# One row sum instead of two in an attention stage: GpSimd adds the DMA engines' partial sum to its own, and waits at the stage borders are split

## The chip, the core and the metric

The kernel runs on one core of a Trainium2 chip. The engines of the core are TensorE (PE, matmuls), VectorE (DVE), ScalarE (ACT), GpSimd (POOL) and SyncE (SP, which here only issues transfers); each works through its own queue in order, and they meet at semaphores. The metric is the device time of one execution in microseconds. Before the change it is 3310.89 us, the median of 3 runs (3309.64 to 3310.94).

## What is computed

```python
x = L0_attn_x                       # (2, 2048, 1024)
xn = _layernorm(x)
q, k, v = xn @ wq, xn @ wk, xn @ wv # 32 heads of 32, 8 key heads, each for 4 query heads
scores = q k^T * 32 ** -0.5, causal
s = (softmax(scores) @ v) @ wo
w = top 2 of 8 experts, softmax(xn @ W_router.T), renormalised
base = xn @ W_base.T + b_base
g = silu(base + 2.0 * sum_e w_e * (xn @ lora_A[e].T) @ lora_B[e].T)
return x + s * g
```

## The kernel before, in words

The 4096 tokens are eight chunks of 512 (CH). Four stages follow each other on one core, and TensorE works in all of them.

1. Constants: a block of its own (L1556) in which POOL makes an identity and two masks and DVE rounds two of them. The next block starts when all engines have left it.
2. Projection (project_programs, L251): for each chunk the weights, split in a high and a low half for accuracy, are multiplied with the turned tokens (three products, L596 to L598), v and router first, then eight q products, two k products and one for the adapters. The results go through DRAM. During the last chunk the first score products of the attention stage are mixed in (scores_to, maxima_to and move_rows; SCORES_OF is how many for each product, LEAD = 84 in all). load_ahead (L1156) fetches the first k, v and q for it.
3. Attention: 16 groups (a batch and a key head with its four query heads), each with chunks c = 0 to 3 of 512 queries. In chunk c there are 4(c+1) tiles of 128 keys, j. A table (EVENTS, L166, filled by rule for each tile) sets the order of the work on all engines alike: PE multiplies scores twice, once with queries in rows for the maxima ("S", L1284, row_max on DVE, a group ahead), once with keys in rows for the exponentials ("T", L1380; ACT writes probs, L1441). "W" multiplies probs with v (L1335).
   The sum of the exponentials over the keys is formed in three ways. ADDS (L145) lists the tiles that POOL adds into added (L1249, op "A"); DMA_ADDS (L146) lists those that a DMA with an add sums into dma_added (L1259, op "D", issued by POOL, each waiting for the landing of the one before); REST names four tiles of chunk 3 that nobody adds. "Y" (row_sums, L1340) lets PE multiply added, dma_added and the rest with ones (L1353) for a chunk's sum. It stands 18 tiles into the next chunk, for chunk 3 behind tile 9 of the next group.
   After Y, ACT copies the sum, SyncE moves it into few columns (L1), DVE inverts it ("I"), SyncE stores (L2, L1213) and spreads it (L3, L1220), POOL multiplies o_sb with it ("N", L1272), and SyncE stores the result (L4, L1225) when the multiply is done. In SyncE's queue L4 of chunk 3 (tile 41 of the next group) stands ahead of L2 and L3 of chunk 0 (tiles 45 and 49).
   The probs live in a ring of 11 buffers; ACT waits for a buffer until its last reader is done.
4. Gate (gate_programs, L654) and output projection (L829). The gate's weights are split by ACT (high, L717) and DVE (low, L756) into gw; first_products (L807) works on the first tokens before the last row sum.

## Time and profile before

| | |
|---|---|
| median of 3 runs | 3310.89 us |
| profiled execution | 3312.78 us, span 3311.0 us |
| PE busy | 3238.1 us (98%) |
| DVE, ACT, POOL busy | 1889.5, 1437.3, 1357.0 us |
| attention stage | about 682 to 2574 us |

Busy time counts instructions of the engine alone, not the ones that issue transfers or wait. A busy PE is not PE at its peak, since matmuls are pipelined and their ends are modelled: the distance between two starts says more than a duration. Idle time of another engine costs nothing by itself; what matters is who waits for whom.

### The profile page before, as it was taken

How to read it: one execution, taken by the hardware profiler on the slowest of the kernel's cores; microseconds unless marked ns; L12 is line 12 of the kernel's file. 1: busy time of each engine (PE TensorE's matmuls, PEld its weight loads, DVE VectorE, ACT ScalarE, POOL GpSimd, SP SyncE). 2: the span in 40 equal slices, each digit the busy share in tenths (PEclk: the TensorE clock that was granted, in tenths of full speed). 3: DMA queues.
4: the chain of work that ended last, by engine and by line, in shares of the span. 5: the costliest groups of instructions: out<-in, count | busy, mean ns of one | idle time of the engine just before them, and what ended most of it. 6: DMA issues, size and time to landing. Idle time of an engine off the chain costs nothing.

```text
span 3311.0 us, 51264 instructions
## 1 busy us (share of the span) xinstructions
PE 3238.1 (98%) x18048; PEld 2193.0 (66%) x18048; DVE 1889.5 (57%) x4622; ACT 1437.3 (43%) x2658; POOL 1357.0 (41%) x549
## 2 busy tenths in 40 slices
PE   6999999999999999999999999999999999999999
PEld 5888888755555555555555555555553788888887
DVE  6333333577777777777777777777773322223333
ACT  3222111056666666666666666666666111010110
POOL 0000000046776776776686677678667000000000
PEclk9999999999999999999999999999999999999999
DMA  6455554556666666566566666666666544445554
GB/s 232 158 163 158 166 159 147 143 119 132 143 137 135 143 130 138 125 142 138 128 145 138 137 136 129 138 132 145 135 162 142 174 140 138 144 156 191 192 199 165
DMA packets 283503, 494.53 MB, mean 149 GB/s; under 512 B 40864, under 2 KB 156576, under 8 KB 263328
## 3 DMA queue, kind: packets, MB, share of 16 engines
q1 hardware_dynamic: 260256, 333.04, 33.7%
q0 software_dynamic: 20736, 151.00, 23.2%
q10 hardware_dynamic: 2304, 7.87, 0.7%
q8 instruction: 113, 1.85, 0.2%
q14 instruction: 94, 0.77, 0.1%
HBM read 205.03 MB, written 134.74 MB: 103 GB/s over the span
## 4 chain that ended last, share of the span: by engine, by line
PE 91%; DVE 4%; ACT 1%; DMA 1%; issue 1%; SPq 1%; POOL 0%; ACTq 0%; DVEq 0%; POOLq 0%
PE cols_ps L1380 16%; PE o_ps L1335 15%; PE rows_ps L1284 14%; PE cols_ps L596 4%; PE cols_ps L598 4%; PE cols_ps L597 4%; PE cols_ps L1353 4%; PE rows_ps L795 4%; PE rows_ps L796 4%; PE rows_ps L797 4%; PE rows_ps L947 4%; PE rows_ps L946 4%; PE rows_ps L945 4%; DVE row_max L1469 2%; PE cols_ps L1383 2%; PE o_ps L596 1%
## 5 line engine op out<-in xcount | busy, mean ns | idle before, releaser
L1249 POOL TENSOR_TENSOR added<-added,probs 128x2048 f32<-128x2048 f32 (+3 forms) x320 | 1171.7, 3661 | 859.2 <-PE o_ps L1335 793.0
L1469 DVE TENSOR_REDUCE row_max<-rows_ps 128x1 f32<-128x512 f32 x1536 | 994.8, 683 | 297.8 <-PE rows_ps L1284 294.7
L1441 ACT ACTIVATE probs<-cols_ps 128x512 f32<-128x512 f32 x1728 | 919.1, 610 | 305.6 <-PE cols_ps L1380 278.6
L1473 DVE CUSTOM_DVE_ANT_0 masked_rows<-rows_ps,tri 128x128 bf16<-128x128 f32 (+3 forms) x1024 | 484.5, 483 | 176.7 <-PE rows_ps L1284 174.1
L1284 PE MATMUL rows_ps<-k_st,q_st 96*128 96x512 f32 (+3 forms) x1536 | 520.7, 362 | 12.8 <-DVE row_max L1469 7.9
L1380 PE MATMUL cols_ps<-q_st,k_st 97*128 97x512 f32 x1248 | 519.8, 423 | 6.7 <-issue 6.1
L1335 PE MATMUL o_ps<-probs,v_st 128*32 128x512 f32 (+3 forms) x4224 | 428.6, 522 | 0.0
L1380 PE MATMUL cols_ps<-q_st_last,k_st 97*128 97x512 f32 x928 | 381.3, 425 | 4.4 <-ACT dma_added L1441 3.2
L1284 PE MATMUL rows_ps<-k_st,q_st_last 96*128 96x512 f32 (+3 forms) x1024 | 364.5, 381 | 2.0
L1380 PEld LDWEIGHTS cols_ps<-q_st,k_st 97*128 97x128 f32 x1248 | 236.7, 190 | 179.7 <-issue 113.0
L1284 PEld LDWEIGHTS rows_ps<-k_st,q_st 96*128 96x128 f32 x1536 | 292.7, 191 | 91.0 <-DVE row_max L1469 36.9
L1380 PEld LDWEIGHTS cols_ps<-q_st_last,k_st 97*128 97x128 f32 x928 | 174.4, 189 | 151.2 <-issue 88.7
L1259 POOL DMA_DIRECT2D dma_added<-probs x144 | 125.8, 874 | 315.6 <-ACT probs L1441 308.3
L1335 PEld LDWEIGHTS o_ps<-probs,v_st 128*32 128x32 f32 x4224 | 111.3, 109 | 209.8 <-issue 145.0
L596 PE MATMUL cols_ps<-xt_hi,w_hi 128*128 128x512 f32 x576 | 231.8, 402 | 0.6 <-DVE logits L531 0.6
L795 PE MATMUL rows_ps<-gw,g_t 128*128 128x512 f32 x576 | 225.1, 391 | 6.6 <-DVE gw L756 5.0
L1284 PEld LDWEIGHTS rows_ps<-k_st,q_st_last 96*128 96x128 f32 x1024 | 194.2, 190 | 53.5 <-DVE row_max L1469 20.5
L598 PE MATMUL cols_ps<-xt_hi,w_lo 128*128 128x512 f32 x576 | 227.7, 395 | 0.0
L597 PE MATMUL cols_ps<-xt_lo,w_hi 128*128 128x512 f32 x576 | 227.3, 395 | 0.0
L797 PE MATMUL rows_ps<-gw,g_t 128*128 128x512 f32 x576 | 224.6, 390 | 0.0
L796 PE MATMUL rows_ps<-gw,g_t 128*128 128x512 f32 x576 | 224.6, 390 | 0.0
L1441 ACT ACTIVATE added<-cols_ps 128x512 f32<-128x512 f32 x256 | 139.3, 599 | 146.4 <-PE cols_ps L1380 109.2
(130 smaller groups left out, 3862.7 us busy)
## 6 DMA issues: line engine op xcount, KB each, us to landing
dma_added<-probs POOLq DMA_DIRECT2D x144, 1024.0 KB, 7.8
q_st<-scratch_q_hi SPq DMA_DIRECT2D x96, 256.0 KB, 6.0
x_sb<-in_x SPq DMA_DIRECT2D x32, 512.0 KB, 4.1
scratch_xt_hi<-xt_hi SPq DMA_DIRECT2D x32, 512.0 KB, 6.0
scratch_xt_lo<-xt_lo SPq DMA_DIRECT2D x32, 512.0 KB, 6.7
scratch_q_hi<-out_hi SPq DMA_DIRECT2D x64, 256.0 KB, 2.5
scratch_q_lo<-out_lo SPq DMA_DIRECT2D x64, 256.0 KB, 2.9
l_sb<-scratch_l_inv SPq DMA_DIRECT2D x256, 64.0 KB, 4.8
```

The costliest lines, as they stand in the source:

```text
L596: nc.tensor.matmul(out, lh, rh, start=(k == 0), stop=False)
L597: nc.tensor.matmul(out, lh, rl, start=False, stop=False)
L598: ins = nc.tensor.matmul(out, ll, rh, start=False, stop=(k == KT - 1))
L795: nc.tensor.matmul(acc[half][:, :], t_hi, w[:, k, 0, cols], start=(k == 0), stop=False)
L796: nc.tensor.matmul(acc[half][:, :], t_hi, w[:, k, 1, cols], start=False, stop=False)
L1249: nc.gpsimd.tensor_tensor(total[:, :, q0:CH], total[:, :, q0:CH], probs_of(c, j)[:, :, q0:CH], ALU.add).then_inc(pool_added, 1)
L1284: nc.tensor.matmul(rows_ps[rows_slot(k)][:, 0:keys], q_st[c][0:K1, h, i * P:(i + 1) * P], k_st[kbuf][0:K1, CH * p:CH * p + keys], start=Tr ...
L1335: ins = nc.tensor.matmul(o_ps[h * HD:(h + 1) * HD, q0:CH], v_st[vbuf][:, j, :], probs_of(cc, j)[:, h, q0:CH], start=(j == 0), stop=(j == s ...
L1380: ins = nc.tensor.matmul(into, k_st[n.u][:, j * P:(j + 1) * P], q_st[c][:, :, i * P:(i + 1) * P], start=True, stop=not diagonal)
L1441: nc.scalar.activation(probs_of(c, j)[:, :, i * P:(i + 1) * P], cols_ps[cols_slot(AT_T[t])][:, :].rearrange("p (h q) -> p h q", h=NREP), A ...
L1469: nc.vector.tensor_reduce(into, bank[:, :], AX.X, ALU.max).then_inc(rows_free, 1)
L1473: nc.vector.tensor_tensor_reduce(masked_rows[rows_slot(k)][:, 0:keys], bank[:, 0:keys], tri[:, CH - keys:CH], 1.0, MASKED, ALU.add, ALU.ma ...
```

## The change

GpSimd gets one more kind of operation, "J": after its last add of a chunk that has DMA adds (chunks 1 to 3), it waits for the last of these to land and adds dma_added to added. PE's row sum no longer reads dma_added. At the borders of the stages waits become finer: the constants are made at the start of the one large block; the first v products are ordered by weight row, each waiting for its own; the last chunk's scores start one product later, nine to a product; v is loaded behind q and the last q before the last stores; PE waits only for the accumulators that the next tiles need; the gate's first products take all high halves before the low ones.

```diff
-SCORES_OF = KT
+SCORES_OF = KT + 1
...
+    if DMA_ADDS[_c]:
+        event(max(tiles_through(_c, ADDS[_c][-1]) - 1, weighed_at(_c, ADDS[_c][0])), "J", _c)
...
-NADD = sum(len(a) - 1 for a in ADDS if a)
+JOINED = [1 if a else 0 for a in DMA_ADDS]
+NADD = sum(len(a) - 1 for a in ADDS) + sum(JOINED)
...
+            def join(n, c, back):
+                total = added[c % 2]
+                added_of, par = dma_adds_through(c, NJG), c % 2
+                pool.wait_ge(dma_done[par], n.lin(16 * NDMA[par], 16 * (added_of - back * NDMA[par])))
+                pool.wait_ge(pool_added, n.lin(NADD, sums_through(c) - 1 - back * NADD))
+                nc.gpsimd.tensor_tensor(total[:, :, :], total[:, :, :], dma_added[par][:, :, :], ALU.add).then_inc(pool_added, 1)
...
-                pe.wait_ge(pool_added, n.lin(NADD, adds_through(cc, NJG) - back * NADD))
+                pe.wait_ge(pool_added, n.lin(NADD, sums_through(cc) - back * NADD))
                 parts = [(added[cc % 2], 0)]
-                if DMA_ADDS[cc]:
-                    added_of, par = dma_adds_through(cc, NJG), cc % 2
-                    pe.wait_ge(dma_done[par], n.lin(16 * NDMA[par], 16 * (added_of - back * NDMA[par])))
-                    parts.append((dma_added[cc % 2], 0))
...
-        pe.wait_ge(w_lo_ready, KT)
...
-                for t in range(TPC):
+                if first_pair and u == 0:
+
+                    pe.wait_ge(acc_free, TPC)
+                    for k in range(KT):
+                        pe.wait_ge(w_lo_ready, k + 1)
...
-                    scored = SCORES_OF * (j - 1)
-                    between = None if ahead or j == 0 else lambda k: scores_to(scored + k + 1)
+                    scored = SCORES_OF * (j - 2)
+                    between = None if ahead or j < 2 else lambda k: scores_to(scored + k + 1)
...
-                load_kv(0, 0)
+                load_k(0, 0)
                 load_q(0, 0)
                 load_q(0, 1)
                 load_q(0, 2)
+                load_v(0, 0)
...
-            pe.wait_ge(project.acc_free, project.acc_free_last)
-            pe.wait_ge(ones_ready, 2)
+            pe.wait_ge(project.acc_free, project.acc_free_last - 2)
+            pe.wait_ge(ones_ready, 1)
...
+                        if n.lin(1) == 0 and t == 2:
+
+                            pe.wait_ge(project.acc_free, project.acc_free_last)
+                        if n.lin(1) == 1 and t == 0:
+                            pe.wait_ge(ones_ready, 2)
...
+        for k in range(NW):
+            pe.wait_ge(w_hi_ready, k + 1)
+            for part in range(2):
+                for half in range(2):
+                    nc.tensor.matmul(acc[half][:, :], tokens[0][:, part, k, :], w[:, k, 0, halves[half]],
+                                     start=(k == 0 and part == 0), stop=False)
         for k in range(NW):
             pe.wait_ge(w_lo_ready, k + 1)
             for half in range(2):
-                ins = step(0, half, k)
+                ins = nc.tensor.matmul(acc[half][:, :], tokens[0][:, 0, k, :], w[:, k, 1, halves[half]], start=False,
+                                       stop=(k == NW - 1))
```

The order on GpSimd's queue at the end of chunk 1 and the start of chunk 2, group 1. Before (added1 and dma_added1 are the partial sums of chunk 1, added0 and dma_added0 those of chunk 2, o_sb3 belongs to chunk 3 of the group before, o_sb0 to chunk 0):

```order
L1249 TENSOR_TENSOR added1<-added1,probs7 128x4x256
L1249 TENSOR_TENSOR added1<-added1,probs8 128x4x128
L1272 TENSOR_TENSOR o_sb3<-o_sb3,l_sb1 128x512
L1259 DMA dma_added0<-probs9 128x2048
L1249 TENSOR_TENSOR added0<-added0,probs10 128x2048
L1272 TENSOR_TENSOR o_sb0<-o_sb0,l_sb0 128x512
L1259 DMA dma_added0<-probs0 128x2048
```

And in the changed kernel, at the same place:

```order
L1332 TENSOR_TENSOR added1<-added1,probs7 128x4x256
L1332 TENSOR_TENSOR added1<-added1,probs8 128x4x128
L1340 TENSOR_TENSOR added1<-added1,dma_added1 128x2048
L1364 TENSOR_TENSOR o_sb3<-o_sb3,l_sb1 128x512
L1349 DMA dma_added0<-probs9 128x2048
L1332 TENSOR_TENSOR added0<-added0,probs10 128x2048
L1364 TENSOR_TENSOR o_sb0<-o_sb0,l_sb0 128x512
L1349 DMA dma_added0<-probs0 128x2048
```

One row is new, the add of dma_added1, and it stands ahead of the multiply of the chunk before and of the first DMA add of the next chunk.

The order on TensorE at the row sum of chunk 3, before (probs7 to probs10 are the four tiles that nobody adds):

```order
L1353 MATMUL cols_ps1<-added1,ones 32x512 x4
L1353 MATMUL cols_ps1<-dma_added1,ones 32x512 x4
L1353 MATMUL cols_ps1<-probs7,ones 32x512 x4
L1353 MATMUL cols_ps1<-probs8,ones 32x384 x4
L1353 MATMUL cols_ps1<-probs9,ones 32x256 x4
L1353 MATMUL cols_ps1<-probs10,ones 32x128 x4
```

And in the changed kernel:

```order
L1443 MATMUL cols_ps1<-added1,ones 32x512 x4
L1443 MATMUL cols_ps1<-probs7,ones 32x512 x4
L1443 MATMUL cols_ps1<-probs8,ones 32x384 x4
L1443 MATMUL cols_ps1<-probs9,ones 32x256 x4
L1443 MATMUL cols_ps1<-probs10,ones 32x128 x4
```

The row on dma_added is gone; the place of the sum among the tiles is the same.

## Rows read from the trace of the kernel before

**Rows 1.** The page, busy time, share and instructions of each engine
```profile
PE 3238.1 (98%) x18048; PEld 2193.0 (66%) x18048; DVE 1889.5 (57%) x4622; ACT 1437.3 (43%) x2658; POOL 1357.0 (41%) x549
```
**Rows 2.** Windows: stretch, length; busy PE, PEld, DVE, ACT, POOL; granted clock; DMA; GB/s
```profile
720.00:2500.00 1780.00, 1760.60 (x10976) 993.05 (x10974) 1341.50 (x3576) 1144.05 (x2186) 1281.97 (x501) 1.00 0.63 137
...
2515.00:2550.00 35.00, 34.05 (x158) 11.29 (x150) 0.25 (x1) 21.96 (x45) 27.18 (x12) 0.91 0.56 118
...
601.00:606.40 5.40, 5.35 (x15) 4.39 (x16) 1.71 (x8) 0.00 (x0) 0.00 (x0) 0.50 1.07 223
```
**Rows 3.** The chain of waits from 720 to 2500 us, by line
```profile
by line: PE cols_ps L1380 27.8%; PE o_ps L1335 27.2%; PE rows_ps L1284 25.2%; PE cols_ps L1353 7.0%; DVE row_max L1469 4.4%; PE cols_ps L1383 3.0%; DVE masked_rows L1473 1.9%; ACT dma_added L1441 1.2%; issue 1.1%; ACT o_sb L1457 0.5%; PE ro
```
**Rows 4.** Timeline, one row sum: start, us, engine, line, operation, operands, count
```profile
729.29 1.04 PE L1353 MATMUL cols_ps<-added,ones 128*32 128x512 f32 x8
...
730.15 1.04 PE L1353 MATMUL cols_ps<-dma_added,ones 128*32 128x512 f32 x8
```
**Rows 5.** Timeline of POOL, group 1; in brackets the idle time before
```profile
834.67 3.82 POOL L1249 TENSOR_TENSOR added<-added,probs 128x1024 f32<-128x1024 f32 x2
838.45 1.28 POOL L1272 TENSOR_TENSOR o_sb<-o_sb,l_sb 128x512 f32<-128x512 f32 x1
...
852.36 1.28 POOL L1272 TENSOR_TENSOR o_sb<-o_sb,l_sb 128x512 f32<-128x512 f32 x1 [4.34 <-ACT probs L1441]
853.58 0.86 POOL L1259 DMA_DIRECT2D dma_added<-probs  x1
...
864.32 12.49 POOL L1249 TENSOR_TENSOR added<-added,probs 128x2048 f32<-128x2048 f32 x4
...
878.01 0.87 POOL L1259 DMA_DIRECT2D dma_added<-probs  x1
...
886.58 0.87 POOL L1259 DMA_DIRECT2D dma_added<-probs  x1 [3.09 <-ACT probs L1441]
...
911.54 4.88 POOL L1249 TENSOR_TENSOR added<-added,probs 128x2048 f32<-128x2048 f32 x1
```
**Rows 6.** Timeline of SyncE's queue, the same group
```profile
839.82 0.36 SPq L1225 DMA_DIRECT2D scratch_o<-o_sb  x1
840.30 0.37 SPq L1213 DMA_DIRECT2D scratch_l_inv<-l_few  x1
843.41 4.16 SPq L1220 DMA_DIRECT2D l_sb<-scratch_l_inv  x4
```
**Rows 7.** Timeline of PE: three row sums begin
```profile
805.94 1.04 PE L1353 MATMUL cols_ps<-added,ones 128*32 128x512 f32 x8
...
881.13 1.04 PE L1353 MATMUL cols_ps<-added,ones 128*32 128x512 f32 x8
...
923.19 1.04 PE L1353 MATMUL cols_ps<-added,ones 128*32 128x512 f32 x8
```
**Rows 8.** Timeline of POOL, group 0
```profile
760.14 0.87 POOL L1259 DMA_DIRECT2D dma_added<-probs  x1 [1.44 <-ACT probs L1441]
...
795.00 4.87 POOL L1249 TENSOR_TENSOR added<-added,probs 128x2048 f32<-128x2048 f32 x1
```
**Rows 9.** The page, DMA issues: count, size, median us to landing
```profile
dma_added<-probs POOLq DMA_DIRECT2D x144, 1024.0 KB, 7.8
```
**Rows 10.** Timeline of SyncE's queue, start
```profile
5.71 1.82 SPq L312 DMA_DIRECT2D x_sb<-in_x  x4
```
**Rows 11.** Timeline of PE, waits at the borders
```profile
49.74 0.50 PE L596 MATMUL cols_ps<-xt_hi,w_hi 128*128 128x512 f32 x1 [0.62 <-DVE logits L531]
...
601.05 0.48 PE L1284 MATMUL rows_ps<-k_st,q_st 96*128 96x128 f32 x1 [4.86 <-DMA q_st<-scratch_q_hi]
...
681.62 0.77 PE L1380 MATMUL cols_ps<-q_st,k_st 97*128 97x512 f32 x1 [6.05 <-issue]
...
2559.32 0.77 PE L795 MATMUL rows_ps<-gw,g_t 128*128 128x512 f32 x1 [5.00 <-DVE gw L756]
```
**Rows 12.** The line's instructions: count, ns min/median/max, first and last start
```profile
L756 DVE TENSOR_TENSOR gw<-gw_raw,gw x9: 1210/1211/5485, 2553.7 to 2567.0; 128x1024 fp32r<-128x1024 f32 x9
```

More of the change, by code:

```diff
@@ L371, in pair_of_chunks @@
                     store_xt(Step(pair, 1) if u == 0 else Step(pair + 1, 0), 1 - u)
+                if last and u == 1:
+                    wait_apart(sp, acc_full, NA * NCH - 1, passed)
+                    wait_apart(sp, xt_stored[1], 16 * 2 * TPC * (NCH // 2 + 1), passed)
+                    load_last()
                 s = (NO * u + NO - 1) % 2
@@ L605, in tensor, with pair_of_chunks @@
             turn(zero, j)
-        pe.wait_ge(w_lo_ready, KT)
-        def pair_of_chunks(pair, b, last):
+        def pair_of_chunks(pair, first_pair, last):
             for u in range(2):
@@ L620, in pair_of_chunks @@
                 pe.wait_ge(turn_free, n.lin(NTR, NTR + 4))
-                for t in range(TPC):
+                if first_pair and u == 0:
+                    pe.wait_ge(acc_free, TPC)
+                    for k in range(KT):
+                        pe.wait_ge(w_lo_ready, k + 1)
+                        (wh, wl) = weights(k, C_V, C_Q)
+                        for t in range(TPC):
+                            (th, tl) = tokens(k, t * P, (t + 1) * P)
+                            into = acc[t][:, C_V:C_Q]
+                            nc.tensor.matmul(into, th, wh, start=(k == 0), stop=False)
+                            nc.tensor.matmul(into, th, wl, start=False, stop=False)
+                            ins = nc.tensor.matmul(into, tl, wh, start=False, stop=(k == KT - 1))
+                            if k == KT - 1:
+                                ins.then_inc(acc_full, 1)
+                for t in () if first_pair and u == 0 else range(TPC):
                     pe.wait_ge(acc_free, n.lin(NA, t + 1))
@@ L636, in pair_of_chunks @@
                         turn(m, j)
-                    if not ahead and j > 0:
+                    if not ahead and j > 1:
                         scores_to(scored + SCORES_OF)
@@ L647, in pair_of_chunks @@
                 ins.then_inc(acc_full, 1)
-        over_chunks(pe, pair_of_chunks)
-    Project = namedtuple("Project", "sync gpsimd scalar vector tensor acc_free acc_free_last acc_hi acc_hi_last")
-    return Project(sync, gpsimd, scalar, vector, tensor, acc_free, NA * NCH + 4, acc_hi, NA * NCH)
+        pair_of_chunks(0, True, False)
+        with pe.Fori(1, 3) as pair:
+            pair_of_chunks(pair, False, False)
+        pair_of_chunks(3, False, True)
+    Project = namedtuple("Project", "sync all_stored gpsimd scalar vector tensor acc_free acc_free_last acc_hi acc_hi_last")
+    return Project(sync, all_stored, gpsimd, scalar, vector, tensor, acc_free, NA * NCH + 4, acc_hi, NA * NCH)
 def gate_programs(nc, ctx, sc, wo, b_base, w_raw, w, ow_raw, ow_hi, ow_lo, tokens, bias, z, th, g, acc, passed):
@@ L809, in first_products @@
         pe.wait_ge(t_loaded[0], 64)
+        halves = [slice(half * HALF, (half + 1) * HALF) for half in range(2)]
+        for k in range(NW):
[4 more added lines that the diff above has]
+                                     start=(k == 0 and part == 0), stop=False)
         for k in range(NW):
@@ L1057, in all_stages @@
         NW = KT + 1
+        made = sem("made")
+        rounded = sem("rounded")
+        constants = constants_programs(nc, ident, ident_r, plain_ji, mask_ji, tri, made, rounded)
         project = project_programs(nc, ctx, x, wall, sc, ident, work, small, cols_ps + [o_ps], rows_ps)
@@ L1160, in load_ahead @@
                 load_q(0, 2)
+                load_v(0, 0)
             moved = [0]
             def move_rows(end):
-                for k in FIRST_ROWS[moved[0]:end]:
+                for k in FIRST_ROWS[moved[0]:max(end, 0)]:
                     if ROWS[k][0] == "M":
@@ L1168, in move_rows, with load_last @@
                 moved[0] = max(moved[0], min(end, len(FIRST_ROWS)))
-            project.sync(sp, load_ahead, move_rows)
+            def load_last():
+                load_q(0, CPB - 1)
+            project.sync(sp, load_ahead, move_rows, load_last)
             assert moved[0] >= max(i for i, k in enumerate(FIRST_ROWS) if ROWS[k][0] == "M")
@@ L1184, in run @@
                             wait_apart(sp, probs_ready, made_count(n, c - 1, 0, NJG) if c else n.lin(NUG, 0), passed)
-                        if c == 0 or not last_group:
+                        if c == 0 and n.lin(1) == 1:
+                            project.all_stored(sp)
+                        if c == 0 and n.lin(1) == 0:
+                            pass
+                        elif c == 0 or not last_group:
                             load_q(n.lin(1, 0 if c == 0 else 1), (c - 1) % CPB)
@@ L1265, in run @@
                         add(n, *op[1:])
+                    elif op[0] == "J":
+                        join(n, *op[1:])
                     elif op[0] == "D":
@@ L1273, in run @@
                             .then_inc(norm_ready, 1)
+            constants.gpsimd(pool)
             project.gpsimd(pool)
@@ L1297, in scores_to @@
             def scores_to(end):
-                for k in FIRST_ROWS[scored[0]:end]:
+                for k in FIRST_ROWS[scored[0]:max(end, 0)]:
                     free = rows_free_count(None, 0, k) if k >= NROWS else None
@@ L1493, in maxima_to @@
             def maxima_to(end):
-                for k in FIRST_ROWS[done[0]:end]:
+                for k in FIRST_ROWS[done[0]:max(end, 0)]:
                     count = rows_count(None, 0, k)
@@ L1504, in maxima_to @@
                 done[0] = max(done[0], min(end, len(FIRST_ROWS)))
+            constants.vector(dve)
             project.vector(dve, begin_maxima, maxima_to)
```

65 lines of the change are left out of this document (35 added, 30 removed).

## The prediction

> **What bounds the kernel now.** I read the page's busy shares first [rows 1], then the stages by windows, the chain of waits, and last GpSimd's, SyncE's and TensorE's own timelines. TensorE (PE) is busy 98% of the span. In the attention stage it is busy 1760.6 of 1780 us [rows 2], and the chain of waits lies on its products for over 90% of that stretch [rows 3]. So work taken off PE there is worth its full time, if nothing else becomes late. GpSimd (POOL) looks half idle (41%), and that is misleading: its idle time lies in holes between links of a chain. Below I follow one of the 16 groups through its chunks 1 to 3, because the change loads exactly that engine.
>
> **What is removed.** After a row sum's eight records on `added` come eight on `dma_added`, 729.29 then 730.15 [rows 4]: 0.86 us per part. The engine is never idle there, so nothing hides the part. Chunks 1 to 3 of 16 groups have such a part, 48 sums: 48 x 0.86 = 41.3 us off PE.
>
> **What is added.** 48 joins of 128x2048 on POOL. The same form of add takes 4.6 us: four adds of 2048, 1536, 1024 and 512 elements, two and a half of them in work, take 12.49 us, the row at 864.32 [rows 5]; I keep 4.57. 48 x 4.6 = 220 us on an engine that is busy 1357 of 3311 us [rows 1]: it fits in total. The question is what is queued behind each join, and for that I retime group 1 of [rows 5], in the clock of before:
>
> Join of chunk 1: the adds end at 838.5, the last DMA add of the chunk, issued 8.4 us before that, has just landed (7.8 us in the median) [rows 9], so the join runs 838.8 to 843.4. Behind it on POOL stands the multiply of o_sb of the chunk before (838.45), now done at 844.6 instead of 839.7. SyncE's queue waits for that multiply: its store went out at 839.82, and behind it in the same queue stand the store of the inverse sums (840.30) and the spread of them (843.41) [rows 6]. All three move by some 5 us. The spread feeds the next multiply on POOL (852.36), where POOL already sits idle 4.34 us (the row names probs, but in its queue it is the multiply that waits for the spread); this becomes 857.2. The multiply blocks the DMA add at 853.58, now 858.4, so 4.85 us late. From 853.58 to 876.8 POOL is gapless, so all of it arrives.
>
> Join of chunk 2: runs 881.8 to 886.3, while TensorE comes to that sum at 881.13, less the 0.86 saved before it [rows 7]. PE waits about 5.5 us. Then the multiply, then chunk 3's first DMA add, at 887.6 instead of 878.01.
>
> Join of chunk 3: here POOL and the DMA adds are one chain, each DMA add waiting for the landing of the one before (878.01 and 7.8 to land, and 0.8 to be noticed, give 886.58), with adds filling the rest; the adds end at 916.4, 38.4 us after that first DMA add. Started at 887.6, they end at 926.0 and the join at 930.7. TensorE comes to the sum at 923.19 - 1.7 saved + 5.5 already waited = 927.0. It waits another 3 us or more.
>
> So group 1 saves 2.6 us and waits some 8. It is a bad one. In other groups the spread has slack before it is needed. Done in the same way for all 15 groups that have a successor, the two waits together come to 1.1 us in the mildest and 8.2 in the worst, 74 us in sum. A rough control: chunk 3's adds end on average 6.7 us before their sum begins (in the first 6.1: add from 795.00, sum at 805.94 [rows 7, 8]; over the 15 groups 4.4 to 8.1). Against that stand the join 4.6, the push by chunk 2's join (4.6 less the 1.44 us of idle time at 760.14 [rows 8]) 3.1, the sums that come 1.7 earlier, and the push from chunk 1 through SyncE, between 0 and 4.9, say 2.3 on average: 11.7 - 6.7 = 5.0 a group, 75 us. Bounds: 0 if the joins find holes, 38 if the push through SyncE does not reach POOL, 105 if each DMA add lands 0.5 us later than its median of 7.8 [rows 9]. I take 74, since all terms come from rows of this very chain. Attention stage: -41.3 + 74 = +33 us.
>
> The Trainium skill (DMA: Bandwidth & Descriptors, Anatomy of one DMA) fits such a transfer as 2 us plus bytes at 436 GB/s, by my estimate 4.4 us for 1 MB. The row says 7.8, so by the page chunk 3's chain would have 6 us more slack and the sum would come out near the second rival.
>
> **The start.** SyncE's first load stands at 5.71 us [rows 10], behind the block of the constants. Without that block it can go out at about 1.4 us, 4.3 us earlier; DVE's two copies of constants still end before the tokens land. The first weights are multiplied as they arrive, but the next product waits for DVE's logits, at 49.74 [rows 11], and DVE is busy with the split of the weights and the statistics whatever PE does. So this earlier work gains nothing, and PE then idles about 9 us, after which its granted clock is at the low level, as it was for the 5.4 us behind the 4.86 us wait at 601 (0.50 of full, 1.2 GHz) [rows 2, 11]: that stretch cost about 2.4 us. Net -2.0, bounds -4.3 and 0.
>
> **Border to attention.** PE waited 4.86 us for q_st at 601.05 and then ran until 606.4 at the low clock [rows 2, 11], 2.4 us lost. With the scores one product (5.5 us) later and k and q loaded before v, both go: -7.2 (bounds -7.2 and -4). The 81 scores now share 9 products instead of 10, DVE's load per product rises to some 7.2 of 7.4 us: just hidden. Next, PE's 6.05 us before 681.62 [rows 11]: it may start two tiles at once, but then needs DVE to free the score banks, and DVE has the last low half and a memset of one row of k_st in front of that, until about 681.5; it is late next. I take -2 (bounds -6 and 0).
>
> **Border to the gate.** PE waited 5.0 us for the first low part of gw [rows 11] and then had a stretch of low clock like the one at 601, but shorter; I put it at 1.5 us lost. That first subtraction took 5485 ns where its like take 1211 [rows 12]: it stood still until POOL's add ended. With the high halves first PE has 8.3 us of work without it. But now POOL has, after its late add, another multiply, add and join, 10.6 us, and DVE 9 subtractions, 10.9 us; if they exclude each other, both are over only near 2579, where the sum of chunk 3 began at 2573.2. I take +3 (bounds -7 and +6).
>
> The Trainium skill (SBUF — State Buffer, Who interferes with whom) calls the shared port an exclusive lock between a GpSimd read and a DVE instruction with two SBUF inputs; the 5485 ns agree. By it the saving here is given back; without it the term would be -6.
>
> **Sum.** -41.3 + 74 - 2.0 - 7.2 - 2.0 + 3 = +24.5 us on the profiled execution (span 3311.0, whole 3312.78): 3337. The median of the runs is 1.9 us lower: 3335.4, say 3336.
>
> **The rivals.**
> 1. The joins are hidden. For it speaks POOL's 41%; against it the 6.7 us of slack against a join of 4.6 with 3.1 in front. -41.3 - 8.2 = 3261. Chance 8%.
> 2. On the other side, one mechanism: only chunk 3's chain is late, the push through SyncE's queue does not reach POOL's DMA adds, since the spread lands sooner once it no longer meets other transfers. The waits are then 38.6 us; from below 49.5 us in sum the kernel is faster than before. -41.3 + 38.6 - 8.2 = 3300. Against it: the 4.34 us hole in front of 852.36. Chance 22%.
> 3. As forecast, and TensorE's clock falls at the longer waits. In the last group, with less than 1 us of PE idle in 35, the granted clock averaged 0.91 [rows 2], so 9% of full speed was lost there without a long wait. Some 25 waits at 0 to 2.4 us (the loss at 601) are 0 to 60 us; a third is 20 us, 3356. Chance 13%.
> 4. Waits of 45 to 57 us in sum, neither case clean: 3310, no change. Chance 9%.
>
> **The numbers.** The forecast has 48%, its own range 3318 to 3356. A change under 0.2% (6.6 us) can't be told from none. Faster: 8 + 19 of the second rival = 27%. Same: 10%. Slower: 63%. The range 3290 to 3366 leaves out the first rival and the far end of the third.
>
> **What would show it.** A PE wait released by `added` in front of the row sums of chunk 2 and above all chunk 3, some 5 us a group, absent at chunks 0 and 1. The distance from POOL's first DMA add of chunk 3 to the end of its adds still near 38 us, and the multiply behind the join of chunk 1 about 5 us later against the adds. PE's row-sum records 384 fewer. A group's period, 117.25 us now, near 119.5. At 601 no wait; the first load 4.3 us earlier. Wrong would be a period of 114.7 (rival 1), or a wait on DVE or ACT in place of the one on POOL.

## The result, and the profile after

The changed kernel takes 3364.1 us (median of 4 runs, 3360.9 to 3368.7), the kernel before 3310.9 in the same session: ratio 1.0161, 95% interval 1.0147 to 1.0175. The forecast was 3336, slower by 25; it is slower by 53. The direction was right and the size was not; of the waits, which the forecast put above all at chunk 3, 48.8 us stand at chunk 2 and 14.2 at chunk 3. The profiled execution took 3368.7 us, its span is 3366.9 against 3311.0, so 55.9 us are to be explained.

The page first: busy time, share and instructions of each engine, and the start of the chain that ended last, by engine.

```profile
PE 3238.3 (96%) x17664; PEld 2199.7 (65%) x17664; DVE 1896.5 (56%) x4622; ACT 1439.7 (43%) x2658; POOL 1576.9 (47%) x597
...
PE 74%; POOL 11%; DMA 6%; issue 4%; DVE 3%; ACT 2%; SPq 0%; ACTq 0%; POOLq 0%; DVEq 0%
...
L1340 POOL TENSOR_TENSOR added<-added,dma_added 128x2048 f32<-128x2048 f32 x48 | 219.8, 4580 | 12.2 <-DMA dma_added<-probs 5.9
```

TensorE has 384 instructions fewer and yet the same busy time as before [rows 1]; stretches of low clock, below, gave back what the removed ones took off. Of the chain it was 91% before, now GpSimd and the DMA engines hold 17% of it. The join is as long as forecast, 4.58 us.

The attention stage, by windows (stretch, length, busy PE, PEld, DVE, ACT, POOL, granted clock, DMA share, GB/s), and the largest waits of TensorE and of GpSimd's multiply in the same stretch (sum in us, times, longest).

```profile
720.00:2500.00 1780.00, 1699.66 (x10276) 971.33 (x10279) 1303.52 (x3481) 1111.82 (x2117) 1448.15 (x530) 0.98 0.62 132
```
```profile
POOL o_sb L1364 <- DMA l_sb<-scratch_l_inv: 70.1, 12, 7.5
PE cols_ps L1443 <- POOL added L1340: 61.4, 23, 5.6
```

Against [rows 2] TensorE stands 61 us more, all of it in front of the joined sums, and its mean clock is 0.98, not 1.00. GpSimd, the engine that is late, itself stands 70 us in front of its multiply and waits there for the spread. Group 1 on GpSimd, SyncE and TensorE (start, length, engine, line; in brackets the idle time before):

```profile
835.07 4.59 POOL L1340 TENSOR_TENSOR added<-added,dma_added 128x2048 f32<-128x2048 f32 x1 [1.24 <-DMA dma_added<-probs]
839.62 1.29 POOL L1364 TENSOR_TENSOR o_sb<-o_sb,l_sb 128x512 f32<-128x512 f32 x1
840.85 0.85 POOL L1349 DMA_DIRECT2D dma_added<-probs  x1
...
853.15 1.27 POOL L1364 TENSOR_TENSOR o_sb<-o_sb,l_sb 128x512 f32<-128x512 f32 x1 [6.84 <-DMA l_sb<-scratch_l_inv]
...
877.74 4.49 POOL L1340 TENSOR_TENSOR added<-added,dma_added 128x2048 f32<-128x2048 f32 x1
...
921.04 4.60 POOL L1340 TENSOR_TENSOR added<-added,dma_added 128x2048 f32<-128x2048 f32 x1
```
```profile
841.01 0.36 SPq L1308 DMA_DIRECT2D scratch_o<-o_sb  x1
841.48 0.45 SPq L1296 DMA_DIRECT2D scratch_l_inv<-l_few  x1
848.61 2.82 SPq L1303 DMA_DIRECT2D l_sb<-scratch_l_inv  x4
```
```profile
844.16 1.04 PE L1443 MATMUL cols_ps<-added,ones 128*32 128x512 f32 x8
...
882.38 1.93 PE L1443 MATMUL cols_ps<-added,ones 128*32 128x512 f32 x8 [4.35 <-POOL added L1340]
...
925.82 1.04 PE L1443 MATMUL cols_ps<-added,ones 128*32 128x512 f32 x8
```

The forecast chain can be read off link by link: join, multiply, SyncE's store, the store of the inverse sums, the spread, the multiply of chunk 0, the adds, the join of chunk 2, TensorE's wait. One link is new. The store of the inverse sums (8 KB) needs 7 us to land (the spread behind it goes out at 848.61); before it needed 3 (840.30 to 843.41, [rows 6]).

The 55.9 us by stretches, read from the start of the same TensorE instruction in both traces:

| stretch | forecast | measured |
|---|---|---|
| start, to the second turning of tokens (55.40, now 54.30) | -2.0 | -1.1 |
| TensorE at 345 to 352 us | 0 | +5.9 |
| border to attention, to the first row sum (707.10, now 702.51) | -9.2 | -9.4 |
| first row sum to that of the last group (1759.5, now 1814.3 us) | +35.3 | +54.8 |
| last group with the border to the gate (106.6, now 112.8 us) | +0.4 | +6.1 |
| the rest | 0 | -0.4 |

The forecast's -41.3 and 74 stand in the fourth line but for the last group's 2.6 us. A group's period is the time from a row sum to the same one of the next group. Its mean over 15 groups, cut at the row sums, shows where:

| from row sum to row sum | before | after | forecast for after |
|---|---|---|---|
| chunk 0 to 1 | 22.19 | 22.18 | 22.19 |
| chunk 1 to 2 | 34.53 | 37.02 | 35.58 |
| chunk 2 to 3 | 42.07 | 43.85 | 44.26 |
| chunk 3 to 0 | 18.52 | 17.91 | 17.66 |
| period | 117.30 | 120.95 | 119.7 |

(The last column, as the 119.7, is my retiming behind the 74 us, which puts 29 of them at chunk 2 and 46 at chunk 3. The prediction gives only their sum, and 119.5 for the period.) The excess is at chunk 2: 1.44 us a group, 22 us.

### The profile page after: what moved, and what is told of

Read it like the earlier page. It is cut to its first block, busy times and chain, and to the rows that moved or that the text cites. A ratio compares the mean times of both kernels' runs of the same rounds, so it can differ in the third digit from the quotient of the medians.

```text
span 3366.9 us, 50579 instructions
## 1 busy us (share of the span) xinstructions
PE 3238.3 (96%) x17664; PEld 2199.7 (65%) x17664; DVE 1896.5 (56%) x4622; ACT 1439.7 (43%) x2658; POOL 1576.9 (47%) x597
## 4 chain that ended last, share of the span: by engine, by line
PE 74%; POOL 11%; DMA 6%; issue 4%; DVE 3%; ACT 2%; SPq 0%; ACTq 0%; POOLq 0%; DVEq 0%
PE cols_ps L1475 11%; PE o_ps L1429 10%; PE rows_ps L1377 10%; POOL added L1332 8%; PE cols_ps L638 5%; PE cols_ps L640 4%; PE cols_ps L639 4%; PE rows_ps L853 4%; PE rows_ps L854 4%; PE rows_ps L855 4%; PE rows_ps L1011 3%; PE rows_ps L1013 3%; PE rows_ps L1012 3%; DMA dma_added<-probs 3%; PE cols_ps L1443 3%
## 5 line engine op out<-in xcount | busy, mean ns | idle before, releaser
L1332 POOL TENSOR_TENSOR added<-added,probs 128x2048 f32<-128x2048 f32 (+3 forms) x320 | 1189.0, 3716 | 721.7 <-PE o_ps L1429 689.0
L1377 PE MATMUL rows_ps<-k_st,q_st 96*128 96x512 f32 (+3 forms) x1536 | 528.7, 369 | 10.5 <-DVE row_max L1564 10.2
L1475 PE MATMUL cols_ps<-q_st_last,k_st 97*128 97x512 f32 x928 | 393.0, 439 | 4.3 <-ACT dma_added L1536 3.0
L1377 PEld LDWEIGHTS rows_ps<-k_st,q_st 96*128 96x128 f32 x1536 | 300.9, 196 | 85.0 <-DVE row_max L1564 35.1
L1475 PEld LDWEIGHTS cols_ps<-q_st_last,k_st 97*128 97x128 f32 x928 | 182.8, 198 | 162.5 <-issue 99.9
L1340 POOL TENSOR_TENSOR added<-added,dma_added 128x2048 f32<-128x2048 f32 x48 | 219.8, 4580 | 12.2 <-DMA dma_added<-probs 5.9
L853 PE MATMUL rows_ps<-gw,g_t 128*128 128x512 f32 x558 | 217.4, 390 | 1.9 <-DVE g_z L818 1.0
L855 PE MATMUL rows_ps<-gw,g_t 128*128 128x512 f32 x558 | 217.3, 389 | 0.0
L854 PE MATMUL rows_ps<-gw,g_t 128*128 128x512 f32 x558 | 217.3, 389 | 0.0
```

Of the source, the lines that this page charges most:

```text
L853: nc.tensor.matmul(acc[half][:, :], t_hi, w[:, k, 0, cols], start=(k == 0), stop=False)
L854: nc.tensor.matmul(acc[half][:, :], t_hi, w[:, k, 1, cols], start=False, stop=False)
L1332: nc.gpsimd.tensor_tensor(total[:, :, q0:CH], total[:, :, q0:CH], probs_of(c, j)[:, :, q0:CH], ALU.add).then_inc(pool_added, 1)
L1377: nc.tensor.matmul(rows_ps[rows_slot(k)][:, 0:keys], q_st[c][0:K1, h, i * P:(i + 1) * P], k_st[kbuf][0:K1, CH * p:CH * p + keys], start=Tr ...
L1475: ins = nc.tensor.matmul(into, k_st[n.u][:, j * P:(j + 1) * P], q_st[c][:, :, i * P:(i + 1) * P], start=True, stop=not diagonal)
```

## The experiments

All times are medians, and each ratio is taken to the kernel before in the same session. The waits are TensorE's on GpSimd in front of the row sums, over 16 groups. From "pairs written out" down, every kernel also has the exchange of "join 1 behind multiply", and all but the last have the pairs written out; "store 2 in the next group" also has the multiply of chunk 2 behind join 3, and "row sum 3 alone later" builds on it. The edits are shown shortened; where a chunk is not joined, TensorE's second sum and its wait for the DMA adds come back with it.

| kernel | us | ratio to before | waits at chunk 2 / 3, us in sum | period |
|---|---|---|---|---|
| changed | 3364.1 | 1.0161 | 48.8 / 14.2 | 120.95 |
| borders only | 3299.7 | 0.9960 | 0 / 0 | 117.29 |
| joins only | 3372.8 | 1.0172 | 54.4 / 10.8 | 121.11 |
| waits filled | 3376.8 | 1.0187 | 8.3 / 3.4 | 121.44 |
| chunk 2's wait filled | 3366.6 | 1.0172 | 22.2 / 23.4 | 120.85 |
| join 1 behind multiply | 3295.7 | 0.9948 | 2.1 / 16.1 | 116.26 |
| store 3 behind spread 0 | 3299.1 | 0.9968 | 3.1 / 21.3 | 116.61 |
| no join 1 | 3303.6 | 0.9974 | 0.2 / 14.5 | 116.94 |
| pairs written out | 3295.5 | 0.9958 | 3.1 / 21.2 | 116.84 |
| multiply 2 behind join 3 | 3388.8 | 1.0239 | 4.1 / 7.5 | 123.09 |
| store 2 in the next group | 3278.9 | 0.9902 | 2.9 / 8.0 | 115.66 |
| row sum 3 one tile later | 3366.2 | 1.0162 | 53.5 / 4.7 | 121.38 |
| row sum 3 alone later | 3281.8 | 0.9912 | 3.3 / 2.9 | 115.97 |
| joins 1 and 2 | 3276.5 | 0.9895 | 2.0 / 0 | 115.80 |
| joins 1 and 2, with the loop | 3279.9 | 0.9907 | 3.4 / 0 | 115.82 |

The 95% intervals are 0.0013 to 0.0016 to either side (0.0009 for no join 1).

### The joins apart from the rest

```
 # borders only: no chunk is joined
-    if DMA_ADDS[_c]:
-        event(..., "J", _c)
+                if DMA_ADDS[cc]:
+                    pe.wait_ge(dma_done[par], ...)
+                    parts.append((dma_added[cc % 2], 0))
```

> The changed kernel without the three joins of a group: TensorE multiplies both sums again, everything at the start and at the borders stays as changed. Theory (the joins and the waits behind them are the loss, the rest is small): -1.1 us at the start, +5.9 at TensorE's loop back at 345 us, -9.4 at the border to attention, about -3 at the border to the gate, so 3303 us (3299 to 3308), no wait of TensorE on GpSimd in the attention stage and its granted clock there back near 1.00. Rival (the edits at the borders bring the lower clock or cost time by themselves): 3325 us or more, with periods of low clock in the attention stage.

3299.7 us, 11 us less than before (ratio interval 0.9946 to 0.9973), and its granted clock in the attention stage is 1.00:

```profile
720.00:2500.00 1780.00, 1759.82 (x10969) 991.87 (x10969) 1337.93 (x3568) 1143.19 (x2186) 1287.03 (x502) 1.00 0.63 137
```

So the edits at start and borders gain, and the joins alone cost 64 us on top. The opposite kernel:

```
 # joins only: the kernel before, with
+    if DMA_ADDS[_c]:
+        event(max(tiles_through(_c, ADDS[_c][-1]) - 1, weighed_at(_c, ADDS[_c][0])), "J", _c)
-                    parts.append((dma_added[cc % 2], 0))
```

> The kernel before with the three joins of a group and nothing else of the change. Theory: -41.3 us of products, +68 of waits, +33 of low clock: 3370 us (3362 to 3378), with the same waits of TensorE on GpSimd in front of the row sums of chunks 2 and 3. Rival (half of the loss comes from the other edits): 3335 to 3345.

3372.8 us: as the theory had it. The two kernels also give the border to the gate as a table of four, from the last group's first row sum to its last: 106.6 us before, 99.2 with the borders alone, 115.8 with the joins alone, 112.8 with both. The high halves ahead of the low ones gain 7.4 us without joins; the joins take 9.2 with the old order and 13.6 with the new. In the joins' kernel TensorE waits twice for DVE's low halves, 7.73 us and later 2.51, and DVE stands still:

```profile
2619.64 0.77 PE L803 MATMUL rows_ps<-gw,g_t 128*128 128x512 f32 x1 [7.73 <-DVE gw L764]
```

In the changed kernel two of the nine subtractions are long, 6.45 and 5.61 us against 1.21. They stand beside GpSimd's last add and its join, and the second ends 1.1 us behind the join (the rows of GpSimd, and of DVE with min/median/max in ns):

```profile
2609.37 4.90 POOL L1332 TENSOR_TENSOR added<-added,probs 128x2048 f32<-128x2048 f32 x1
2614.42 5.40 POOL L1340 TENSOR_TENSOR added<-added,dma_added 128x2048 f32<-128x2048 f32 x1
```
```profile
L814 DVE TENSOR_TENSOR gw<-gw_raw,gw x9: 1209/1210/6450, 2608.9 to 2627.6; 128x1024 fp32r<-128x1024 f32 x9
```

### Does the clock fall because TensorE stands still?

```
 # waits filled: 16 at chunk 2, 6 at chunk 3
+                for _ in range((0, 0, 16, 6)[cc]):
+                    nc.tensor.matmul(bank, ident_r, mask_ji, start=True, stop=True)
                 pe.wait_ge(pool_added, ...)
```

> The changed kernel; in front of the wait for the joined sum TensorE multiplies a constant into the bank that the row sum then overwrites, 16 products of 0.23 us (3.7 us) at chunk 2 and 6 (1.4 us) at chunk 3: 81 us more work, most of it in time in which TensorE stood still. Theory (the clock falls because TensorE stood still): the periods of low clock in the attention stage shrink from about 99 us to under 30, and the kernel gets faster although it does more: 3364 - 33 + 18 for fill beyond the waits = 3349 (3338 to 3360). Rival (the clock falls for another reason, the load of the other engines or the mix of products): low clock as before, 3364 + 18 = 3382 (3374 to 3390).

The mean granted clock over the span answers the first half. The rows are of the changed kernel, of this one and of the kernel before:

```profile
core 0: 3366.9 us, clock 0.981
```
```profile
core 0: 3376.7 us, clock 0.993
```
```profile
core 0: 3311.0 us, clock 0.994
```

At the level of 1.2 GHz TensorE thus spent about 3366.9 x 0.019 x 2 = 128 us in the changed kernel, 47 here and 40 before. (Half of the 88 us between changed and before, 44 us by this estimate, is about the busy time that the removed instructions took off.) Added up over the stretches of the attention stage with a granted clock of 0.50 it is 75 us in the changed kernel and 7 here; one of these stretches of the changed kernel begins 1 us ahead of the end of the wait at 882.38:

```profile
881.30:887.90 6.60, 5.52 (x17) 3.32 (x18) 2.19 (x5) 2.44 (x5) 6.60 (x4) 0.50 0.58 134
```

With TensorE at work in the waits the low clock is nearly gone, so it comes from standing still, not from the load of other engines. But the time did not fall: 3376.8, 28 us above what I expected. From the first product of the fill to the row sum it is 94 us in 15 groups, where the waits alone had been 61. The fill was too large to tell, so a smaller one:

```
+                for _ in range((0, 0, 8, 0)[cc]):
```

> The changed kernel with 8 products of a constant (8 x 0.238 = 1.9 us) in front of the wait for the joined sum of chunk 2, where 13 of the 16 waits are 2.2 us or longer; 30 us more of work, nearly all of it inside the waits. Theory (standing still brings the low clock): low clock in the attention stage falls from 75 us to 20 to 45, and the kernel gets faster with the work added: 3364 - 12 = 3352 us (3343 to 3358). Rival (the clock falls for another reason, or the remaining 2 us of the long waits are enough for it): 3362 to 3372.

```profile
core 0: 3360.7 us, clock 0.992
```
```profile
871.41 2.11 PE L1439 MATMUL cols_ps<-mask_ji,ident_r 128*128 128x512 f32 x8
...
874.85 1.07 PE L1446 MATMUL cols_ps<-added,ones 128*32 128x512 f32 x8 [1.33 <-POOL added L1340]
```

3366.6 us, in the rival's range, though its reason is wrong: the low clock did fall, to 3360.7 x 0.008 x 2 = 54 us in all. What stayed was the period, 120.85. The waits at chunk 3 grew from 14.2 to 23.4 us. From the end of the join of chunk 2 to the end of the join of chunk 3 GpSimd and the DMA adds need 43.4 us in the changed kernel (882.23 to 925.64 in group 1), and TensorE starts both sums behind these joins. From chunk 2 to chunk 3 both filled kernels take 43.35 us, the changed one 43.85. So the lower clock after a wait costs only 0.5 us a group there: the rest of it lies in time in which TensorE would wait at chunk 3. It is a symptom much more than a term of the sum.

### The way through SyncE's queue

```
 # join 1 behind multiply: same tile, the other order on GpSimd
-    if DMA_ADDS[_c]: event(..., "J", _c)      # ahead of the loop with "N"
+    if DMA_ADDS[_c]: event(..., "J", _c)      # behind it
```

> The changed kernel with one pair of GpSimd's instructions exchanged: the join of chunk 1 comes behind the multiply of chunk 3 of the group before, not ahead of it. Theory (the push goes through that multiply, SyncE's store of its result and the spread queued behind the store): SyncE's store, the spread and the multiply of chunk 0 come 3 to 4.6 us earlier, GpSimd's idle time in front of that multiply (6.8 us in group 1) is filled by the join; the waits at chunk 2 fall from 49 us in sum to 10 to 15, those at chunk 3 grow from 19 to 20 to 30, the loss by the clock halves: 3364 - 31 - 16 = 3317 (3302 to 3335). Rival (the 4.6 us of the join themselves make chunk 2 late, wherever it stands): 3358 to 3366.

3295.7 us, 68 us less than the changed kernel by exchanging two neighbouring instructions, and faster than before. Expected were 3317. In group 1:

```profile
831.71 1.29 POOL L1365 TENSOR_TENSOR o_sb<-o_sb,l_sb 128x512 f32<-128x512 f32 x1
833.31 4.58 POOL L1341 TENSOR_TENSOR added<-added,dma_added 128x2048 f32<-128x2048 f32 x1 [0.31 <-DMA dma_added<-probs]
837.84 0.87 POOL L1350 DMA_DIRECT2D dma_added<-probs  x1
...
843.43 1.29 POOL L1365 TENSOR_TENSOR o_sb<-o_sb,l_sb 128x512 f32<-128x512 f32 x1
```
```profile
833.09 0.36 SPq L1309 DMA_DIRECT2D scratch_o<-o_sb  x1
834.41 0.34 SPq L1297 DMA_DIRECT2D scratch_l_inv<-l_few  x1
836.68 1.72 SPq L1304 DMA_DIRECT2D l_sb<-scratch_l_inv  x4
```

The small store is back ahead of the DMA add (834.41 and 837.84), the spread goes out 2.3 us behind it, and the multiply of chunk 0 finds its data without idle time. Over groups 1 to 14, in us:

| | store of inverse sums lands after | spread lands after | GpSimd idle in front of the multiply |
|---|---|---|---|
| before | 2.46 | 6.96 | 1.57 |
| changed | 7.11 | 3.72 | 6.08 |
| join 1 behind multiply | 2.39 | 5.35 | 0.62 |
| store 3 behind spread 0 | 2.03 | 3.70 | 0.00 |

In the changed kernel the store is issued 0.6 to 1.0 us behind GpSimd's DMA add of 1 MB in 13 of the 14 groups, and there it lands 0.2 to 0.3 us behind that add's landing (group 1: issued 840.85 and 841.48, landed 848.33 and 848.53). In the other, group 13, it is issued only 0.40 us behind and lands after 2.5 us, 5 us ahead of the add. Before, the DMA add came 1.6 to 3.6 us behind the store:

```profile
841.91 0.88 POOL L1259 DMA_DIRECT2D dma_added<-probs  x1 [2.18 <-ACT probs L1441]
```

The Trainium skill (DMA: Bandwidth & Descriptors, Queues, rings and completion order) says that the increment of a semaphore lands only after every earlier write of the same DMA engine, across its queues. The traces agree from some distance on. In all 16 kept traces together, 616 stores of inverse sums are issued 0.59 us or more behind a DMA add that is still under way, and each lands 0.16 to 2.3 us behind it; 11 are issued at most 0.43 us behind, and each lands ahead of it. The result's store of 256 KB shows the same: in group 1 it goes out at 841.01, 0.16 us behind the add, and lands after 2.5 us. GpSimd's instruction that issues the add takes 0.85 us, so the start of an issue need not be where the add takes its place in the order; what sets the limit between 0.43 and 0.59 us was not tested. That the order on GpSimd itself is not what helped is shown by the next kernel, which leaves it and moves one store on SyncE.

```
 # store 3 behind spread 0
-    event(_t + 32, "L4", _c)
+    event(_t + (41 if _c == CPB - 1 else 32), "L4", _c)
```

> The changed kernel with GpSimd's order as changed (join of chunk 1 ahead of the multiply of chunk 3); on SyncE alone the store of that multiply's result comes behind the inverse sums' store and spread of chunk 0, not ahead of them. Theory (the push goes through SyncE's queue): the store of the inverse sums goes out at about 834.5 in group 1 instead of 841.5, ahead of GpSimd's DMA add at 840.9, lands in about 2.5 us instead of 7.1 (median), the multiply of chunk 0 finds its spread there; waits at chunk 2 under 12 us in sum (48.8), at chunk 3 15 to 25, low clock in the attention stage under 20 us (75): 3308 us (3298 to 3322), a little above the exchange on GpSimd. Rival (the order on GpSimd itself is what helped): 3350 or more.

3299.1 us; the wait for the spread is gone from 70 us to almost nothing, with the join still ahead of the multiply:

```profile
828.56 0.34 SPq L1296 DMA_DIRECT2D scratch_l_inv<-l_few  x1
830.31 1.71 SPq L1303 DMA_DIRECT2D l_sb<-scratch_l_inv  x4
```
```profile
PE cols_ps L1443 <- POOL added L1340: 24.4, 18, 3.1
...
POOL o_sb L1364 <- DMA l_sb<-scratch_l_inv: 0.7, 1, 0.7
```

```
 # no join 1
-    if DMA_ADDS[_c]:
+    if _c in (2, 3):
```

> The changed kernel without the join of chunk 1 alone; TensorE multiplies both sums there again (13.8 us), the joins of chunks 2 and 3 stay. Theory (the join of chunk 1 pushes the rest and brings most of the waits): 3295.7 of the exchange on GpSimd + 13.8 - 2 = 3307 us (3299 to 3316), waits at chunk 2 near 0. Rival (each of the three joins has an equal part of the loss of 95 us): 3364 - 32 + 14 = 3346 (3338 to 3354).

3303.6 us. One join of three removed takes the waits at chunk 2 away, although TensorE does 13.8 us more.

### The jump at 345 us

```
 # pairs written out
-        with pe.Fori(1, 3) as pair:
-            pair_of_chunks(pair, False, False)
+        pair_of_chunks(1, False, False)
+        pair_of_chunks(2, False, False)
```

> As the exchange on GpSimd (3295.7), and TensorE's second and third pair of chunks in the first stage stand written out one behind the other, not in a loop. Theory (the 1.7 and 2.2 us of idle time at 347 and 351 us and the low clock behind them are the loop's jump back): no idle time there, 3295.7 - 5.6 = 3290 us (3287 to 3293). Rival (they come from the stores of the tokens or from DVE): idle time stays, 3294 to 3298.

In the changed kernel TensorE stands still where its loop over pairs of chunks jumps back:

```profile
347.55 0.38 PE L638 MATMUL cols_ps<-w_hi,xt_hi 128*128 128x264 f32 x1 [1.71 <-DVE hw L612]
...
351.57 0.28 PE L639 MATMUL cols_ps<-w_lo,xt_hi 128*128 128x264 f32 x1 [2.20 <-issue]
```

Two packets of the queue that loads instructions fall into 344 to 352 us, among transfers that fill the DMA engines (queue, packets, MB, share of 16 engines):

```profile
q1 hardware_dynamic: 4452, 2.25, 99.9%
q8 instruction: 2, 0.03, 1.4%
```

Before, the loop jumped back at 190 us, also beside token stores, and there was neither a packet of that queue nor idle time. Written out, both idle times are gone and the first row sum comes 4.5 us earlier (695.6 for 700.1), though two packets of that queue fall into the same stretch there too, beside DMA engines as full:

```profile
q8 instruction: 2, 0.03, 0.4%
```

Yet the median is the same, 3295.5, and not the 3290 of the theory: the waits at chunk 3 in this profile are 5 us larger. Runs of this kernel lie 7 us apart, so I repeated it in reverse in a kernel that hardly waits:

> The kernel with the joins of chunks 1 and 2 (3276.5) with TensorE's second and third pair of chunks in a loop again, as in the changed kernel. Theory (the jump back costs its idle time and the low clock behind it): 1.7 + 2.2 us of idle time at 347 us again, 3276.5 + 5 = 3281.5 us (3279.5 to 3284). Rival (the idle time is taken from slack elsewhere): 3275 to 3278.

3279.9 against 3276.5, and the first row sum at 699.0 against 695.7: the jump costs about 3.3 us there. The two medians are of two sessions and the intervals of their ratios overlap, so the distance in the traces is the firmer number. Which part of the jump TensorE waits for stays open: the two packets were read from their place in time alone, and without the loop two of them left no idle time (their transfers took 0.4% of the engines' time there, 1.4% with the loop).

### The last wait, at chunk 3

```
 # multiply 2 behind join 3
-    event(_t + 26, "N", _c)
-    event(_t + 32, "L4", _c)
+    if _c != 2: event(_t + 26, "N", _c)
+    event(_t + (35 if _c == 2 else 32), "L4", _c)
+event(weighed_at(3, 2) + 30, "N", 2)        # behind "J", 3
```

> As the kernel with the pairs written out, and the multiply of chunk 2 on GpSimd, which now stands among the last adds of chunk 3, comes behind the join of chunk 3 (its store on SyncE three tiles later). Theory (chunk 3's chain of adds and join sets TensorE's last waits, 16 us in sum, about 1 us a group): the join ends 1.3 us earlier, the waits at chunk 3 shrink to about 4 us: 3290 - 12 = 3278 us (3273 to 3284). Rival (the later multiply and store hold back SyncE's queue or the chain does not get shorter, since the DMA adds set it): 3289 to 3296.

3388.8 us, the worst of all, by the same mistake that the change makes. SyncE's store now waits for the later multiply, and the loads of q stand behind the store:

```profile
1040.88 0.36 SPq L1311 DMA_DIRECT2D scratch_o<-o_sb  x1
1041.35 0.66 SPq L1207 DMA_DIRECT2D q_st_last<-scratch_q_hi  x1
```
```profile
PE rows_ps L1380 <- DMA q_st_last<-scratch_q_hi: 51.7, 14, 4.8
```
```profile
core 0: 3387.0 us, clock 0.975
```

The waits at chunk 3 did shrink as wanted, from 21.2 to 7.5 us, and the low clock follows a wait for a load just as it followed those for GpSimd: 3387.0 x 0.025 x 2 = 169 us. With the store moved past the loads:

```
+    event(_t + (48 if _c == 2 else 32), "L4", _c)
```

> As the kernel with the multiply of chunk 2 behind the join of chunk 3, but SyncE's store of that multiply's result stands eight tiles into the next group, behind the loads of q, not ahead of them. Theory (the 93 us lost there were SyncE's queue standing at the store, the loads of q behind it, TensorE's 14 waits for q and the low clock behind these): the waits for q are gone, low clock under 15 us instead of 133, and what was looked for shows: waits at chunk 3 under 10 us in sum (21 with the multiply ahead): 3281 us (3275 to 3287). Rival (the multiply behind the join holds up something else, or the chain of DMA adds alone sets the end): 3292 or more.

3278.9 us, as expected: 110 us less for one store's place in a queue (a wait of the last group, tied to that store, moves with it). Two tries to give the row sum more time:

```
 # row sum 3 one tile later
+    _t += (0, 0, 0, 1)[_c]
```

> As the exchange on GpSimd with the pairs written out (3295.5), with the row sum of chunk 3 and what follows from it one tile (0.86 us) later in every queue. Theory (TensorE waits there 1.4 us in the mean): each wait shrinks by 0.86 us, in sum 21 to 9, and the low clock behind them with it: 3283 us (3278 to 3289). Rival (ScalarE's first write of chunk 1 into the same buffer now waits for the row sum and hands the delay back to TensorE): 3293 or more.

3366.2 us, neither theory. The edit also moved the multiply of chunk 3 to the next tile, behind the join of chunk 1 once more, and the waits at chunk 2 are back (53.5 us). It says nothing on its own question, but repeats the main finding. The row sum alone:

```
-    event(_t, "Y", _c)
+    event(_t + (1 if _c == CPB - 1 else 0), "Y", _c)
```

> As the kernel with the store of chunk 2 in the next group (3278.9), with the row sum of chunk 3 alone one tile later on TensorE; GpSimd's and SyncE's orders stay. Theory: its waits (8 us in sum) fall to about 1: 3273 us (3269 to 3277). Rival (ScalarE's first write of chunk 1 goes into the buffer that this sum reads, waits for it and holds up TensorE's tiles): 3280 or more.

3281.8 us, in the rival's range, though TensorE's waits fall from 11 to 6 us. (Against the 3278.9 the intervals of the ratios overlap; the period is 115.97 for 115.66.) ScalarE now stands 85 us in front of the buffer until the row sum has read it, a wait that the kernel without the edit does not have:

```profile
ACT added L1539 <- PE cols_ps L1446: 84.6, 15, 6.2
```

That is the rival's first half. The second, that the delay comes back to TensorE, is not shown: TensorE's own waits on ScalarE are the same in both traces.

Last, the join of chunk 3 left out:

```
-    if DMA_ADDS[_c]:
+    if _c in (1, 2):
```

> As the exchange on GpSimd with the pairs written out (3295.5), without the join of chunk 3: TensorE multiplies both sums there, 13.8 us. Theory (the join of chunk 3 is what ends late, 21 us of waits): waits at chunk 3 under 3 us, 3295.5 + 13.8 - 20 - 4 of clock = 3285 us (3281 to 3291). Rival (chunk 3's adds themselves end late behind the join of chunk 2, with or without a join of their own): 3298 or more.

3276.5 us, the fastest, ratio 0.9895 (0.988 to 0.9911); expected were 3285. TensorE pays the 13.8 us of chunk 3's second sum and hardly waits:

```profile
PE cols_ps L1449 <- POOL added L1342: 1.9, 3, 0.9
```

It beats the kernel before by 35 us and the changed one by 88.

## Why the prediction was right in direction and wrong in size

**The removal, right.** 384 instructions less, 0.86 us a part: between the row sums of chunks 2 and 3 "joins 1 and 2, with the loop" takes 41.23 us where it multiplies both sums at chunk 3 but not at chunk 2, 0.84 less than 42.07.

**The chain of group 1, right in its links but one.** Join 4.59 (forecast 4.6), wait at chunk 2 4.35 us (5.5), sum of all waits in 15 groups 61 to 66 us, depending on whether the 0.2 us by which neighbouring instructions overlap are counted, against 74. Two readings in the prediction do not carry their numbers: 12.49 us for two and a half adds is 5.0 each, and the 4.57 is that of single adds elsewhere in the trace; and a join that ends at 886.3 against a sum that comes at 880.3 is a wait of 6.0, not 5.5. From the end of the join of chunk 2 to that of chunk 3 it is 43.4 us (forecast 886.3 to 930.7, 44.4), which let TensorE through without a wait at chunk 3 in this group, since it came there at a lower clock. The rivals "hidden" and "only chunk 3" are out; the push through SyncE's queue is not one part among others but nearly all: without it (store 3 behind spread 0) the kernel is faster than before.

**The step that failed** is the sentence "In other groups the spread has slack before it is needed", and with it the 2.3 us a group that I took for the push from chunk 1, "between 0 and 4.9". I moved the store and the spread in time and let each keep the landing time that it had before. But the later store changes places with GpSimd's DMA add, and then lands with it, 7.1 us for 2.5. In the changed kernel no group has slack: GpSimd stands 3.6 to 8.1 us in front of the multiply in groups 1 to 14. The push itself measures 4.5 us in the mean (1.3 to 7.2) where I had 2.3: the DMA add behind the multiply of chunk 0 is issued 9.2 us behind the row sum of chunk 1 in the mean of these groups, before 4.7 (and 4.4 with join 1 behind the multiply, 4.6 without join 1). At chunk 2, where the retiming had 29 us of waits, there are 49. This is 22 of the 31 us that were missing; about 6 are the jump at 345 us, 6 the border to the gate, and -2 the rest.

**The third rival, the clock** (0 to 60 us) named a real thing: low clock after the waits, some 75 us of it in the attention stage. It was not the cause of the miss. Filling the waits removed it and the period stayed; it took the place of waits at chunk 3, which are 14 us where I had 46. Chunk 2 to chunk 3 came out 0.4 us a group below my retiming, not above it. Elsewhere (chunk 3 to 0) it costs 0.25 us a group.

**The jump at 345 us, missed.** I had looked at the moved products and not at the loop that they left behind: 5.9 us in this trace.

**The borders.** To attention: -9.4 for -9.2, and the wait at 601 is gone; of the second one 2.27 us stay, released by DVE as expected. At the start: -1.1 for -2.0, the first load 4.3 us earlier and 12.26 us idle in front of DVE's logits, where about 9 were forecast.

```profile
46.09 0.80 PE L638 MATMUL cols_ps<-xt_hi,w_hi 128*128 128x512 f32 x1 [12.26 <-DVE logits L573]
...
679.24 1.39 PE L1377 MATMUL rows_ps<-k_st,q_st 96*128 96x512 f32 x2 [2.27 <-DVE row_max L1564]
```

To the gate: +3 was forecast, with bounds of -7 and +6; the last group with this border measures 6.1 and the 2.6 us of products removed there, 8.7, outside the bounds. The direction came from the exclusion of GpSimd and DVE, which holds; the join's own part, up to 13.6 us in the last group, was too small in my sum. The low clock is part of it: it stood at 0.51 beside full work right behind the wait at 2575.78.

```profile
2577.80:2584.60 6.80, 6.80 (x23) 2.36 (x24) 0.10 (x1) 3.64 (x8) 4.45 (x1) 0.51 0.91 196
```

## What to carry to other kernels

When a step is moved later on one engine, look for what it now falls behind on the others: the order in which two queues reach the DMA engines is part of the critical path, and a small transfer issued from some 0.6 us behind a large one lands with the large one. Retime a chain with landing times taken again for the new order, not with those of the old trace. An instruction on an in-order queue that waits for the moved step (here a store nobody needed soon) belongs behind everything that others wait for. Moving that store turned a loss of 53 us into a gain of 12, and exchanging join and multiply into one of 17; the gain of 35 also needed the pairs written out and the join of chunk 3 left out.

## What was not expected of the hardware

- A store of 8 KB issued 0.6 to 1.0 us behind a 1 MB DMA add lands 7.0 to 9.2 us after its issue, within 0.3 us of the add (13 of 14 groups); 0.4 us behind it (the other group) or 1.6 to 3.6 us ahead of it, it takes 2.5. Over all traces the limit lies between 0.43 and 0.59 us, with no exception among 627 stores.
- TensorE's clock at the lower level behind waits of 2 to 5 us costs much less than it shows, when the next wait would have taken up the time: 31 us instead of 75 at that level in the attention stage, and the period moved from 120.95 to 120.85.
- A jump back of TensorE's loop left 1.7 and 2.2 us idle where two packets of instructions were loaded beside DMA engines at 99.9%, and none at 190 us in the kernel before, where none were loaded. Two packets in the same stretch without the jump left no idle time either.
